# Cross attention: the probabilities of the context keys from scores computed a second time, instead of by turning them

## The reference, cut to what matters

```
scores = jnp.maximum(q @ k.T * inv_sqrt_d + attention_mask, finfo.min)
attn_output = softmax(scores) @ v                       # 112 own keys
a_scores = softmax(q @ a_k.T * inv_sqrt_d)              # 375 context keys
attn_output = attn_output + tanh(gate) * a_scores @ a_v
return attn_output @ Wo
```

## Time and profile before

| | |
|---|---|
| Median of 3 runs | 1815.8 us (1813.87 to 1819.28) |
| The profiled execution | 1809.46 us, of which the span (first to last instruction) is 1807.7 |
| TensorE busy | 1743.7 us, 96% of the span |
| TensorE weight loads | 1155.4 us, 64% |
| VectorE busy | 979.6 us, 54% |
| ScalarE busy | 609.9 us, 34% |
| GpSimd busy | 406.5 us, 22% |
| Mean granted clock of TensorE | 0.991 of full speed |
| Cross attention | from about 406 us to about 943 us |

### The profile page before, as it was taken

One profiled execution on the slowest core, in us unless ns is written; L12 is line 12 of the kernel. 1 busy time (PEld: TensorE's weight loads), 2 busy tenths in 40 slices (PEclk: granted clock), 3 DMA queues, 4 the chain that ended last, 5 costly groups with the idle time before them and its releaser, 6 DMA issues.

```text
span 1807.7 us, 31468 instructions
## 1 busy us (share of the span) xinstructions
PE 1743.7 (96%) x12998; PEld 1155.4 (64%) x12998; DVE 979.6 (54%) x1865; ACT 609.9 (34%) x1934; POOL 406.5 (22%) x485
## 2 busy tenths in 40 slices
PE   7999999999999999999999999998999999999998
PEld 6776666646566665665665888886587765444444
DVE  3775656427656566666744111116555555665887
ACT  1242222316655555555740111110422223332411
POOL 2532222512020120120003000005142220002576
PEclk9999999999999999999999999999999999999999
DMA  9100002000000000000215988877000031762001
GB/s 397 37 1 1 1 1 111 1 10 18 18 18 18 2 18 18 2 18 2 117 48 206 390 331 327 332 266 258 1 1 1 2 120 68 276 197 96 17 24 41
DMA packets 31838, 172.36 MB, mean 95 GB/s; under 512 B 4008, under 2 KB 4008, under 8 KB 17904
## 3 DMA queue, kind: packets, MB, share of 16 engines
q1 hardware_dynamic: 29456, 163.01, 24.0%
q0 software_dynamic: 2240, 7.34, 1.2%
HBM read 155.66 MB, written 16.52 MB: 95 GB/s over the span
## 4 chain that ended last, share of the span: by engine, by line
PE 86%; DVE 9%; POOL 3%; ACT 2%; issue 1%; DMA 0%; POOLq 0%; DVEq 0%; SPq 0%; ACTq 0%
PE PS L1209 8%; PE PS L1001 6%; PE PS L1356 6%; PE PS L1052 5%; PE PS L1278 5%; PE PS L1086 5%; PE PS L1125 4%; PE PS L1077 4%; PE PS L1387 4%; PE PS L1218 4%; PE PS L1323 3%; PE PS L1109 3%; PE PS L1374 3%; PE PS L1145 2%; PE PS L1060 2%; PE PS L1040 2%
## 5 line engine op out<-in xcount | busy, mean ns | idle before, releaser
L2159 POOL TENSOR_TENSOR rstd<-veps,mhalf 128x1 f32<-128x1 f32 (+1 forms) x71 | 53.7, 757 | 498.2 <-DVE veps L1417 475.0
L1209 PEld LDWEIGHTS PS<-R,W 128*128 128x128 f32 x1344 | 153.2, 192 | 11.7 <-issue 11.7
L1541 DVE TENSOR_REDUCE nmx<-PS 112x2 f32<-112x750 f32 x128 | 114.3, 933 | 77.9 <-PE PS L1109 77.5
L1209 PE MATMUL PS<-R,W 128*128 128x128 f32 x1344 | 153.6, 275 | 2.2 <-DVE R L1713 2.2
L2012 ACT ACTIVATE R<-PS,nmx 112x375 f32<-112x375 f32 x256 | 142.9, 575 | 4.1 <-DVE nmx L1541 4.1
L1001 PE MATMUL PS<-xT,W 128*128 128x224 f32 x640 | 127.6, 360 | 0.9 <-ACT xT L1943 0.7
L1001 PEld LDWEIGHTS PS<-xT,W 128*128 128x128 f32 x640 | 122.4, 194 | 9.1 <-issue 6.9
L1720 DVE TENSOR_TENSOR R<-R,PS 128x512 f32<-128x512 f32 x21 | 14.4, 687 | 199.1 <-PE PS L1209 199.1
L1356 PE MATMUL PS<-W 128*128 128x512 f32 x256 | 117.5, 602 | 0.0
L1125 PEld LDWEIGHTS PS<-cst,R 112*125 112x125 f32 x768 | 90.1, 191 | 22.0 <-issue 17.5
L1387 PE MATMUL PS<-W,xT 128*128 128x512 f32 x224 | 100.7, 593 | 1.9 <-ACT xT L1953 1.9
(11 more groups left out here) (301 smaller groups left out, 3230.1 us busy)
## 6 DMA issues: line engine op xcount, KB each, us to landing
W<-in_we SPq DMA_DIRECT2D x63, 1024.0 KB, 7.8
W<-in_entwT SPq DMA_DIRECT2D x8, 1024.0 KB, 7.3
W<-in_entpw SPq DMA_DIRECT2D x8, 1024.0 KB, 8.9
W<-in_ctxT SPq DMA_DIRECT2D x8, 750.0 KB, 4.2
R<-in_ctxT SPq DMA_DIRECT2D x8, 750.0 KB, 9.9
R<-in_ctx SPq DMA_DIRECT2D x8, 750.0 KB
xs_rows<-in_x SPq DMA_DIRECT2D x3, 1792.0 KB, 36.4
R<-xs_rows SPq DMA_DIRECT2D x21, 256.0 KB, 8.3
```

The lines of the kernel that those rows point to most:

```text
L1209: o = e.matmul(PS[:, m, c * 128:(c + 1) * 128], gate_up(j % 3, k, off + c * 128), BT[:, j % 2, k, :], start=k == 0, stop=k == 3)
L1541: e.tensor_reduce(nmx[0:S, par, r:r + 2], PS[0:S, r:r + 2, 0:SC], AX.X, ALU.max, negate=True).then_inc(*up("cmax", (b, c, par, r)))
```

## The change

The context probabilities are no longer turned. Instead:

- xc and cm stay, but only for the maxima. cm writes the negated maxima into nmw, each in the column of a partition that the query of this par doesn't use (16 - 16 par in each strip). mt, new, turns nmw by one transpose, and VectorE adds the result to QM in place. The keys KcT are held twice, once for each par; in the same partition each has ones in place of keys (ScalarE writes them with a scale `keep` and a bias `unit`). The product of query and keys is then the score minus its maximum.
- xk, new, computes the scores again with keys on partitions: for each par 12 matmuls (3 groups of 125 keys, 4 strips) over 32 rows, with 125 columns of weights and 112 moving columns, in banks 0 to 3. ce takes the exponential of two strips at once (672 elements), with no bias and no sum. xcv reads its result directly.
- xct and its copies, xr, xb, and the sum of xm piece 3 are gone. The columns of VX and Vc that were zero are one (`padding`), so xv and xcv give the sums of the probabilities in the partitions of the other head of the strip; even and odd heads have columns of their own in bank 7.
- xd now runs for each (b, c): VectorE gathers the sums (a multiply and a multiply-add), swaps the halves of each strip (stream_shuffle) and takes 224 reciprocals; GpSimd masks the numerators and adds them. xn, new, multiplies and adds on VectorE.
- All key copies are ScalarE's, two for each ck. Both copies of xt are ScalarE's.
- The order: the ring of a (b, c) is now four slots, with ck and cv cut into halves of two matmuls as smaller fill, and SHARE says how fill is divided. mt of par 1 stands behind the first fill item of the fourth slot.

```diff
-COST = {..., "ck": 2.55, "cv": 3.5, "xs": 0.45, "xc": 0.65, "xt": 0.42, "xct": 0.45,
-        "xv": 0.25, "xcv": 0.25, "xr": 0.2, "xb": 1.8, "xw": 3.5,
+COST = {..., "ck": 1.28, "ck1": 1.28, "cv": 1.75, "cv1": 1.75, "xs": 0.6, "xc": 0.85, "xk": 0.8, "mt": 0.12, "xt": 0.45,
+        "xv": 0.25, "xcv": 0.75, "xw": 3.5,
-GAP = {"own": 3.0, 0: 6.5, 1: 5.0}
+SHARE = (1.5, 1.2, 1.0, 1.5)
 def attendx():
+    out = []
+    for n in range(4 * NBATCH + 2):
+        here, last, past = (pieces_of(m) for m in (n, n - 1, n - 2))
+        a, b_, c_, d = [], [], [], []
+        if here:
+            a += [("xs", *here)] + [("xm", *here, k) for k in range(2)]
+        if last:
+            a += [("xv", *last, par) for par in range(2)] + [("xcv", *last, 0), ("xk", *last, 1)] + [("ce", *last, 1, r) for r in (0, 2)]
+        if here:
+            a += [("xm", *here, 2), ("xe", *here)]
+            b_ += [("xc", *here, 0)] + [("cm", *here, 0, r) for r in (0, 2)]
+        if past:
+            b_.append(("xn", *past))
+        if last:
+            c_ += [("xcv", *last, 1), ("xu", *last)]
+        if here:
+            c_ += [("xc", *here, 1), ("mt", *here, 0)] + [("cm", *here, 1, r) for r in (0, 2)]
+            d += [("xt", *here, par) for par in range(2)] + [("xk", *here, 0)] + [("ce", *here, 0, r) for r in (0, 2)]
+        if last:
+            d.append(("xd", *last))
+        out += [a, b_, c_, d]
@@ cross()
+        unit = sum(cost(s) for s in fill + late) / (4 * sum(SHARE))
+            out += runs[n]
+            due += unit * SHARE[n % 4]
             some = []
             while fill and (due > cost(fill[0]) / 2 or n == mine[-1]):
+            if n % 4 == 3:
+                some.insert(1, ("mt", *pieces_of(n // 4), 1))
@@ psum_use
     if k == "xc":
-        return (0, 1, 2, 3), 4, [("cexp", (*a, r)) for r in range(4)]
+        return (0, 1, 2, 3), 4, [("cmax", (*a, r)) for r in (0, 0, 2, 2)]
+    if k == "mt":
+        return LOW, 1, [("shifted_q", a)]
+    if k == "xk":
+        return (0, 1, 2, 3), 4, [("cexp", (*a, r)) for r in (0, 0, 2, 2)]
@@ tensor
+            def mt(b, c, par):
+                m = bank(("mt", b, c, par))
+                w.wait_ge(*at("cmax", (b, c, par, 2)))
+                e.transpose(PS[:, m, 0:S], nmw[0:S, par, :], ident[0:S, 0:S]).then_inc(*up("max_turned", (b, c, par)))
+            def xk(b, c, par):
+                w.wait_ge(*at("shifted_q", (b, c, par)))
+                for t in range(3):
+                    for r in range(4):
+                        if t == 0:
+                            free(("xk", b, c, par), r)
+                        o = e.matmul(PS[0:KC, r, bcol(t)], KcT[b % 2][par][ro, c, t * KC:(t + 1) * KC], QM[z][ro, c, par, bcol(i)],
+                                     start=True, stop=True)
@@ vector
+            def xd(b, c):
+                e.tensor_scalar(ND[:, 1, :], OU[:, c % 2, 0, :], high_, None, ALU.mult)
+                e.scalar_tensor_tensor(ND[:, 1, :], OU[:, c % 2, 1, :], low, ND[:, 1, :], ALU.mult, ALU.add)
+                e.stream_shuffle(ND[:, 2, :], ND[:, 1, :], PAIRS)
+                e.reciprocal(ND[:, 2, :], ND[:, 2, :])
+            def xn_(b, c):
+                e.tensor_tensor(ND[:, 1, :], ND[:, 0, :], ND[:, 2, :], ALU.mult)
+                e.scalar_tensor_tensor(OXT[:, c, bcol(b % 2)], ND[:, 1, S:2 * S], tg[:, c:c + 1], ND[:, 1, 0:S], ALU.mult, ALU.add)
@@ scalar
-                    e.activation(p_of(b, c, par)[0:S, r, :], PS[0:S, r, 0:SC], ACT.Exp, bias=nmx[0:S, par, r:r + 1],
-                                 accum_out=sums[0:S, b % 2, n:n + 1]).then_inc(*up("cexp", (b, c, par, r)))
+                e.activation(p_of(b, c, par)[0:KC, r:r + 2, :], PS[0:KC, r:r + 2, 0:3 * S], ACT.Exp).then_inc(
+                    *up("cexp", (b, c, par, r)))
```

More of the change, by code:

```diff
@@ L1 @@
+import itertools
 from contextlib import ExitStack
@@ L241, in context @@
 def context(b):
-    return [("ck", b, c) for c in range(4)] + [("cv", b, t) for t in range(3)]
+    return [(k + z, b, c) for k, n in (("ck", 4), ("cv", 3)) for c in range(n) for z in ("1", "")]
 TASKS = [(b, c, kind) for b in range(NBATCH) for c in range(4) for kind in ("own", 0, 1)]
-GAP = {"own": 3.0, 0: 6.5, 1: 5.0}
[L249 to L256, removed]
@@ L259, in attendx @@
-def attendx():
[L263 to L296, removed]
@@ new lines, with pieces_of @@
+SHARE = (1.5, 1.2, 1.0, 1.5)
+def pieces_of(n):
+    if not 0 <= n < 4 * NBATCH:
+        return None
+    return n // 4, n % 4
+def attendx():
+    out = []
[19 more added lines that the diff above has]
+        out += [a, b_, c_, d]
+    for b in range(1, NBATCH):
+        out[min(16 * (b + 1) + 6, len(out) - 1)] += [("xw", b - 1), ("stats", 2, b - 1)]
+    return out
@@ L321, in cross @@
         late = expert_rows(range(5)) if b == NBATCH - 1 else []
-        mine = range(12 * b, 12 * b + 12)
-        whole = sum(cost(s) for s in fill + late) + sum(cost(s) for n in mine for part in gaps[n] for s in part)
-        unit = whole / sum(GAP[TASKS[n][2]] for n in mine)
+        mine = range(16 * b, 16 * b + 16)
+        unit = sum(cost(s) for s in fill + late) / (4 * sum(SHARE))
         due = 0.0
         for n in mine:
-            if n == mine[2]:
+            if n == mine[3]:
                 fill += late
[L329 to L332, removed]
+            out += runs[n]
+            due += unit * SHARE[n % 4]
             some = []
@@ L336, in cross @@
                 some.append(fill.pop(0))
-            out += head + some + tail
+            if n % 4 == 3:
+                some.insert(1, ("mt", *pieces_of(n // 4), 1))
+            out += some
     h = part(range(5))
[L339 to L342, removed]
+    at_end = {("xk", 7, 3, 1): h[:1], ("xcv", 7, 3, 1): h[1:4], ("xw", 6): h[4:6]}
+    for s in itertools.chain(*runs[16 * NBATCH:]):
+        out += [s] + at_end.get(s, [])
     return out
@@ L480, in build_order @@
     out += spread([s for n in range(4 * NU - 3, 4 * NU + 2) for s in attend0(n)],
-                  norms(1, (3,)) + projectx(0) + turns(1, (3,)) + [("zeros", 0), ("vx", 0)] + [("ck", 0, c) for c in range(4)], pace0)
-    out += [("load", "mask", 0)] + [("cv", 0, t) for t in range(3)] + [("load", "ct", 1)]
+                  norms(1, (3,)) + projectx(0) + turns(1, (3,)) + [("padding", 0), ("vx", 0)] + context(0)[:8], pace0)
+    out += [("load", "mask", 0)] + context(0)[8:] + [("load", "ct", 1)]
     out += cross() + [("scale", 2, 5), ("turn", 2, 5)]
@@ L646, in place @@
         may, count, events = psum_use(step, late)
+        if step[0] in ("ck", "cv"):
+            taken[bank[step][0]], held = n, None
         if not count:
             continue
-        got = list(may) if len(may) == count else sorted(may, key=lambda m: (taken[m], m))[:count]
-        bank[step] = got
+        got = list(may) if len(may) == count else sorted(may, key=lambda m: (m == held, taken[m], m))[:count]
+        if step[0] in ("ck1", "cv1"):
+            held = got[0]
+        bank[step] = bank[{"ck1": "ck", "cv1": "cv"}.get(step[0], step[0]), *step[1:]] = got
         past[step] = [] if group else [frees[m] for m in got if frees[m]]
@@ L945, in program @@
         lp_slot = {s: n % 4 for n, s in enumerate(lps)}
-        pxs = [s for s in order if s[0] in ("xt", "xct")]
-        px_of = {s: PX[n % 6] for n, s in enumerate(pxs)}
+        pxs = [s for s in order if s[0] == "xt"]
+        px_of = {s: PX[n % 4] for n, s in enumerate(pxs)}
         rts = [s[1:] for s in order if s[0] == "pj"]
@@ L1137, in xv @@
                 o.then_inc(*up("values", ("xv", b, c, par)))
-            def xcv(b, c, par, t_):
-                s = ("xct", b, c, par, t_)
-                w.wait_ge(*out_of(s, turned_by(s)))
-                w.wait_ge(*out_of(("cv", b, t_), t_))
-                for r in range(4):
-                    h = (8 * c + 2 * r + par) * 32
-                    o = e.matmul(PS[32 * r:32 * r + 32, 7, bcol(2 * (c % 2) + 1)], Vc[b % 2][0:KC, t_, h:h + 32],
-                                 px_of[s][0:KC, bcol(r)], start=(par, t_) == (0, 0), stop=(par, t_) == (1, 2))
-                o.then_inc(*up("values", ("xcv", b, c, par, t_)))
@@ L1525, in xm @@
                     e.tensor_reduce(sm[:, 0, :], v3, AX.X, ALU.max).then_inc(*up("own_max", (b, c)))
-                elif piece == 3:
-                    w.wait_ge(*at("sexp", (b, c)))
-                    e.tensor_reduce(sums[0:S, b % 2, 8 * c:8 * c + 8], v3, AX.X, ALU.add).then_inc(*up("own_sum", (b, c)))
                 else:
```

283 lines of the change are left out of this document (135 added, 148 removed), and 1 row of the table COST.

## The result

| | before | after |
|---|---|---|
| Median of the runs of one comparison | 1816.53 us (6 runs) | 1799.85 us (6 runs, 1797.15 to 1805.76) |
| Ratio, 95% interval | | 0.9914 [0.9895, 0.9933] |
| Profiled execution | 1809.46 us, span 1807.7 | 1799.19 us, span 1797.3 |
| Mean granted clock | 0.991 | 0.987 |
| xs of the first batch, of the last | 405.8, 870.1 us | 409.2, 862.2 us |

The account below looks back on a forecast made before the run. The prediction took TensorE, busy 96% of the span, as the bound. TensorE work of -37 us, waits of 11, 7.5 in the last batch and -1.5 at the end gave -20 us: 1795 us, range 1768 to 1820.

Parts of the forecast that it names:

- The steps removed and added: TensorE, whole stage: xct, xr, xb save 108 us; xk costs 57 (45 to 105) and mt 8.
- one more switch a piece: TensorE: one more change of array splitting in each of 32 pieces, about 0.2 us each, 6 us.
- the halves: TensorE: context projections cut in halves do the same matmuls, so no cost was counted for them.
- The waits: TensorE in fed batches: small waits of 0.4 us a piece for 28 pieces, 11 us; ends 0 and 1.2 a piece.
- xk of the even heads: Bank turn after xc: comes 3.2 us after it, mt's add and maxima end at 3.15 plus a hand-over, just late.
- Rival D: VectorE's turn passes TensorE's 15.8 us a piece if the reciprocal takes 3 us; slower, about 1840 us; chance 0.13.
- The ring: Banks 0 to 3: five turns a piece instead of three, 12.8 us, shorter than TensorE's 15.8 us a piece.
- Rival C: Ring eats the gain: waits of 1.0 us a piece or xk at 1.1; 1805 to 1820 us; chance 0.17.
- The last batch: Ring of 12.8 us hides the saving: 5 us given back, 2.5 us more by half clock; ends 0 and 15.
- The end of the stage: xr and xb leave a chain mostly hidden by matmuls of the next stage: -1.5 us.
- The sum: Whole kernel: -37 + 11 + 7.5 = -18.5 us, with -1.5 at the stage's end -20 us.

Follow-up runs that it names:

- e4: The changed kernel with the matmuls of every xk issued twice into the same banks; 1837.82 us, ratio 1.013 to the kernel before.
- e1: The changed kernel with the two layer norms ahead of the stage's first maxima moved behind the fourth slot of that piece; 1793.46 us, ratio 0.9893 to the kernel before.
- e5: The changed kernel without the 32 reciprocals of 224 elements, so the output is not normalised; 1796.04 us, ratio 0.9903 to the kernel before.
- e2: The changed kernel with one fill item moved from the other slots to between xcv of the even heads and xk of the odd; 1816.8 us, ratio 1.0018.
- e6: The changed kernel with the context projections ck and cv left whole, each one item of four matmuls; 1839.09 us, ratio 1.0144 to the kernel before.
- e0: The changed kernel run again unedited, as base of the other edits; 1801.14 us, ratio 0.9935 to the kernel before.
- e8: The kernel before with only its context projections ck and cv cut in halves; 1841.96 us, ratio 1.0145 to the kernel before.
- second comparison: The unedited changed kernel measured again against the kernel before; 1801.14 us, ratio 0.9935, 12.8 us faster by the medians.
- e7: e1 with xs and its mask add moved behind mt where the fourth slot has two fill items left; 1796.0 us, ratio 0.9889 to the kernel before.

## Why the prediction was right, point by point

**The steps removed and added** were sized right. In the seven batches stand 54 xct, 6 xb and 6 xr: by the prices of the prediction 89.6 us, measured 91.3. Added are 55 xk at 0.885 and 56 mt at 0.12, 55.4 us; measured 49.1 + 8.9 = 58.0. So -34.2 forecast and -33.3 found (mt was sized low, 0.16 us on the mean for 0.12). That xs gives the price of xk, and not the steps on column strips or the two-strip xb, was the choice that mattered; the pace fits (0.85 to the next start). e4 shows that 0.65 of it is the matmuls and 0.20 comes once a group. If that is the switch, the prediction had it in its 0.885 already and counted it again in the 6 us for one more switch a piece; the halves' 4 to 6 us, which it put at nothing ("do the same matmuls"), took that place. That the two are of one size is luck.

**The waits** come out as sized, and partly where it said. For the mask add it says "just late", and 27 waits of 0.27 us on the mean are there, 7.2 us. At xk of the even heads it says just late too: 1.3 us in all. Forecast for the seven batches 11 for waits and 5.3 for switches, 16.3; found 22.0, and without the first-batch spot (6.6, e1) 15.4. The sum agrees better than its parts: no term of it stood for the halves or for what xv gained. What the prediction had not seen is this spot. It counted VectorE's queue for a steady batch, in which the norms come in other places, and did not go through the first batch, where nothing is behind xc yet and two norms stand ahead of the maxima.

**VectorE**: reciprocal 1.553 us (forecast 1.5), exponentials of 672 elements 0.730 (0.8), maxima 0.933 (0.89), key copies 0.655 to 0.660 (0.5, low by a quarter). 49.4 us of 68 is 11.6 a piece (12.0 said). Rival D needed 15 or more of 15.8; e5 closes it: without its largest new instruction the kernel gains 0.1 to 0.3%.

**The ring.** A piece takes 16.2 us on the mean (453.0 / 28) where it took 16.6; the prediction's 17 and 15.8 came from one stretch of 68 us. Rival C, that five turns of four banks eat the gain, did not happen, but by little: e2 moves one item a piece and loses the whole gain, e6 makes the items coarser and turns 0.9914 into 1.0144. The prediction treats the fill as given ("if the other work is put where it waits"); the fill's grain was the condition on which the sign hung, and C should have been told as that. The Trainium skill, "TensorEngine Tiling (Array Packing)", section "PSUM Bottleneck", says that tiling speeds up TensorE but not the emptying of PSUM. e6 agrees: TensorE waits there for the engines that read its banks, and 38 us are lost; the kernel as changed has few such waits.

**The last batch** gives back less than said: 68.8 to 66.4 us, a gain of 2.4 where 0.6 was left by the sum; it is 67.3 in e0 and 68.8 in e1, so a single trace can't settle this term. Its clock is 0.92 (0.90 before), where the prediction said below 0.9 and 2.5 us lost by it, and TensorE is busy 56.96 of 67 us where it was 65.20 of 69; it waits for VectorE and ScalarE, for instance

```profile
865.92 1.51 PE L1105 MATMUL PS<-W,R 32*112 32x375 f32 x8 [0.86 <-ACT R L1990]
...
875.10 0.63 PE L962 MATMUL PS<-cst,R 128*128 128x128 f32 x4 [2.06 <-DVE R L1417]
...
894.55 0.92 PE L1122 MATMUL PS<-R 32*125 32x112 f32 x24 [1.38 <-DVE R L1504]
```

**Ahead and behind.** The work ahead of the stage was put at nothing and is 3.4 us longer. Every kernel with the cut projections starts its first xs at 406.4 to 411.2 us and has a stretch of half clock at about 360 us; the two executions without the cut start it at 404.5 and 405.8 and have none there. In 355 to 365 us, before and after:

```profile
355.00:365.00 10.00, 6.92 (x107) 4.03 (x109) 5.52 (x10) 3.56 (x16) 3.45 (x5) 1.00 0.01 2
```

```profile
355.00:365.00 10.00, 6.73 (x87) 5.18 (x88) 2.41 (x4) 1.71 (x3) 5.03 (x7) 0.83 0.01 2
```

e8 has it too, so it goes with the cut and not with xk; which waits ahead of it bring it was not tried. The end of the stage, -1.5 by the prediction, gave nothing: behind the last xw stand 868.7 us as before, and 868.6 to 873.4 in the other traces of changed kernels.

**The sum.** Forecast for the seven batches, in the same cut, -17.9 (-34.2 + 5.3 + 11), last batch -0.6, end -1.5: -20. Measured -11.3, -2.4, 0 and +3.4 ahead: -10.3. The term that failed is the queue of VectorE in the first batch (5.7 to 6.6 us, shown by e1) and the one after it is the half clock ahead of the stage (3.4 us), put at nothing. The median is off by less, 1799.85 for 1795, and that is partly luck: both profiled executions of before (1809.5 and 1808.6) lie 7.1 and 6.3 us below the medians of their comparisons and that of after only 0.7, while the forecast took 6.3 us for both kernels. By the second comparison the gain is 12.8 us and not 16.7. What makes the usual execution of before longer than the two traced was not seen.

**The best version** is e1, 0.9893, or e7, the same within its interval: some 20 us (1.1%) below the kernel before. What stands between this and the 33 us of steps are in the main the mask-add waits, the halves, and some 3 us ahead of the stage.

## What to carry to other kernels

When PSUM banks are used more often a piece, first size the filler between two uses, not the engines: here the same steps with filler items of 2.6 to 3.5 us instead of 1.3 to 1.75 turn 0.6 to 0.9% faster into 1.4% slower, although VectorE has a quarter of its time free. A queue that fits in the steady state is to be gone through once more for the first and the last piece: two norms, 4 us of VectorE, cost about as much as all the waits for the mask add in seven batches. And a wait of 0.2 us that is the length of a dependent chain isn't mended by filling in front of it, if the filling is missing elsewhere.

## What the runs showed of the hardware

A group of matmuls on row strips has a part that is paid once: xk takes 0.85 us to the next start, twice the matmuls 1.50, so 0.65 for the matmuls and 0.20 beside them. A pair of xv on column strips takes 0.52 us with row strips behind it and 0.41 with column strips behind it. Both fit what the Trainium skill says in the section "Key Properties" of "TensorEngine Tiling (Array Packing)", that a change of the mode drains TensorE; no run here shows the drain by itself. Cutting a full-array projection in two costs 0.08 us a cut (e6, 3.9 us for 49) to 0.12 (against the kernel before, 6.1 us).

The reciprocal takes 1553 ns for 224 elements a partition beside 203 for 8 and 541 for 64, 6.0 to 6.3 ns an element, while a multiply of the same engine of 112 elements takes 0.27 us. A copy on ScalarE with a scale and a bias per partition takes 655 to 660 ns for 375 elements from PSUM.

The clock fell after short waits of a busy engine: behind 4.06 us of waiting in the first batch (0.86 over 25 us) and behind 1.84 us at four places in e8 (0.70 over 10 us at one). e1 took the first wait away and the half clock went with it. Not every stretch has a wait ahead of it: one in the changed kernel begins at 941.0 us, and TensorE had not waited 0.2 us at once in the 6.8 us before. The same kernel shows other such stretches in each execution: the two of before have 30.6 and 27.2 us of them outside the last 10 us, the two of the change 44.2 and 54.4. At half clock the 8 records of pj took 3.22 us instead of 1.78, so a part of the scatter of single runs is probably this.
